# A fused cross-attention and mixture-of-experts layer: one batch's residual and moments taken apart and placed in two later steps

## The reference

```
ln      = layernorm(layernorm(x))            # x: 16 x 256 x 256, the latents
xn      = layernorm(ctx)                     # ctx: 16 x 256 x 256
q       = ln @ Wq;  k, v = split(concat(xn, ln) @ Wkv)     # 8 heads of 128, 512 keys
x       = x + tanh(g_xattn) * (softmax(q k^T / sqrt(128)) v) @ Wo + bo
h       = layernorm(x)                       # rows of the router and the experts
gates   = h @ Wg;  the two largest of 8, softmax over the two
x       = x + tanh(g_ffn) * sum over the two of w * (silu(h @ W1[e]) @ W2[e])
```

## Time and profile before

| what | value |
|---|---|
| median of 3 runs | 1544.16 us (1540.41 to 1545.47) |
| the profiled execution | 1537.72 us |
| its span, first to last instruction | 1536.0 us |
| busy share PE / PEld / DVE / ACT / POOL | 98% / 90% / 72% / 62% / 39% |
| one batch in the attention stage (8 steps) | 66.4 us, to 0.05 us the same from batch to batch |

### The profile page before, as it was taken

How to read it: one execution, slowest core, us unless ns; L and a number is a source line. 1 busy time by engine, 2 the same in 40 slices (tenths; PEclk the granted TensorE clock), 3 DMA queues, 4 the chain that set the end, 5 groups by cost and what they waited for, 6 DMA issues and landing times. The chain is left out here.

```text
span 1536.0 us, 29968 instructions
## 1 busy us (share of the span) xinstructions
PE 1499.6 (98%) x10446; PEld 1381.2 (90%) x10446; DVE 1112.4 (72%) x2689; ACT 950.0 (62%) x2057; POOL 601.7 (39%) x714
## 2 busy tenths in 40 slices
PE   8999999999999999999999999999889999999997
PEld 6889898898988888898888989888889999999996
DVE  7677777777777777777777777687796666666685
ACT  5555656556565555555565555655787777777775
POOL 5323424333342433434233342233455444444443
PEclk9999999999999999999999999999999999999999
DMA  4000100000000010000000000012855555445563
GB/s 158 10 22 8 22 8 22 28 1 29 8 22 8 22 29 8 22 8 22 8 22 28 8 22 8 8 27 85 227 126 132 129 147 141 129 126 151 136 173 83
DMA packets 57823, 91.13 MB, mean 59 GB/s; under 512 B 8617, under 2 KB 44774, under 8 KB 57550
## 3 DMA queue, kind: packets, MB, share of 16 engines
q1 hardware_dynamic: 41710, 70.19, 14.2%
q0 software_dynamic: 15824, 18.98, 7.0%
q10 hardware_dynamic: 144, 0.05, 0.0%
HBM read 70.91 MB, written 18.29 MB: 58 GB/s over the span
## 5 line engine op out<-in xcount | busy, mean ns | idle before, releaser
L885 POOL TENSOR_SCALAR probs<-probs,rsum 128x512 f32<-128x512 f32 x256 | 174.1, 692 | 532.4 <-DVE rsum L1559 532.2
L1091 ACT ACTIVATE pt_hi<-turn 128x512 fp32r<-128x512 f32 x256 | 139.1, 595 | 238.2 <-PE turn L1239 236.8
L910 POOL DMA_INDIRECT out_rows<-yo,token x71 | 121.6, 1713 | 206.7 <-DMA out_rows<-yo,token 134.5
L1676 DVE TENSOR_TENSOR ht_lo<-hs,ht_hi 128x512 fp32r<-128x512 f32 x142 | 98.2, 691 | 118.1 <-ACT ht_hi L1058 113.3
L1553 DVE TENSOR_REDUCE smax<-score 128x1 f32<-128x512 f32 x256 | 169.6, 684 | 13.1 <-PE score L189 12.7
L992 ACT ACTIVATE probs<-score,nbias 128x512 f32<-128x512 f32 x256 | 173.0, 685 | 3.9 <-DVE nbias L1555 3.8
L1049 ACT ACTIVATE hs<-ph,vecs 128x256 f32<-128x256 f32 (+1 forms) x284 | 114.1, 457 | 93.5 <-PE ph L189 82.4
L1786 DVE TENSOR_TENSOR pt_lo<-turn,pt_hi 128x512 fp32r<-128x512 f32 x256 | 164.1, 682 | 8.3 <-ACT pt_hi L1091 8.1
L187 PE MATMUL py<-w_hi,ht_lo 128*128 (+1 forms) x568 | 162.7, 286 | 3.2 <-DVE ht_lo L1676 3.2
L189 PE MATMUL py<-w_hi,ht_hi 128*128 (+1 forms) x568 | 160.6, 283 | 0.0
L188 PE MATMUL py<-w_lo,ht_hi 128*128 (+1 forms) x568 | 160.5, 283 | 0.0
(11 more groups left out here) (245 smaller groups left out, 4703.2 us busy)
## 6 DMA issues: line engine op xcount, KB each, us to landing
w_raw<-in_L_ffn_W SPq DMA_DIRECT2D x45, 1024.0 KB, 15.6
xhat_rows<-rows SPq DMA_DIRECT2D x16, 264.0 KB, 2.2
x_raw<-in_x SPq DMA_DIRECT2D x16, 256.0 KB, 3.2
c_raw<-in_ctx SPq DMA_DIRECT2D x16, 256.0 KB, 3.3
out_rows<-x SPq DMA_DIRECT2D x16, 256.0 KB, 2.5
xg<-xhat_rows,token POOLq DMA_INDIRECT x71, 4.5
out_rows<-yo,token POOLq DMA_INDIRECT x71
v_raw<-in_L_xattn_Wkv SPq DMA_DIRECT2D x2, 512.0 KB, 8.0
```

What stands on the lines that cost most here:

```text
L885: last = pool.tensor_scalar(probs[n % 2][:, t, :], probs[n % 2][:, t, :], rsum[:, n % 2, t:t + 1], 1.0, ALU.mult, ALU.mult)
L910: pool.indirect_dma_start(out=A["out"], out_offset=bass.IndirectOffsetOnAxis(ap=token[:, u:u + 1].bitcast(U32), axis=0), in_=yo_of(t)[:, s ...
L1091: act.activation(pt[0][:, 2 * t:2 * t + 2, :], turn[t][:, :].rearrange("p (j i) -> p j i", j=2), ACT.Copy).then_inc(s_pthi, 1)
```

## The change

The single function `residual` becomes three: `add_bias` (the sum into `y`), `residual` (the gate, the old `x` and `s_x2`) and `row_moments`. Only `add_bias` stays at the end of step `h == 1`. `residual` goes between `kt_lo` and `qt_lo` of step `h == 2`, `row_moments` to the same place in step `h == 3`. `norm_rows` on POOL goes from behind `normalise` of `h == 1` to behind `normalise` of `h == 3`, ahead of `prepare`. `A_STEP` becomes 4: POOL's `prepare` goes from `h == 3` to `h == 4`; DVE's moments of `x_raw` go from the end of `h == 2` to the end of `h == 3`, because they stand at `A_STEP - 1`, and the moments of `c_raw` from the end of `h == 3` to between `kt_lo` and `qt_lo` of `h == 4`. The last batch, which has no later step, runs the three functions in a row as before. PE's, ACT's and SP's loops are as they were.

```diff
-A_STEP = 3
+A_STEP = 4
 Z_STEP = 2
 R_STEP = 1
 T_STEP = 3
@@ POOL, loop over i, behind normalise(i)
+                if h == T_STEP and 1 <= b < B:
+                    norm_rows(b - 1)
                 if h == A_STEP and b + 2 < B:
                     prepare(b + 2)
                 if h == Z_STEP and b + 1 < B:
                     split_kv(b + 1)
-                if h == R_STEP and 1 <= b < B:
-                    norm_rows(b - 1)
@@ DVE
-            def residual(b):
-
+            def add_bias(b):
                 dve.wait_ge(s_proj, b + 1)
                 dve.tensor_tensor(y[:, :, :], proj[:, :].rearrange("p (t d) -> p t d", t=TT),
                                   bo[:, :].unsqueeze(1).to_broadcast([P, TT, D]), ALU.add)\
                     .then_inc(s_projr, 1)
+
+            def residual(b):
                 dve.wait_ge(s_projr, b + 1)
                 if b >= 2:
                     dve.wait_ge(s_x2st[b % 2], 16 * (b // 2))
                 dve.scalar_tensor_tensor(out=x2[b % 2][:, :, :], in0=y[:, :, :], scalar=tgate[:, 0:1],
                                          in1=x_raw[b % 3][:, :, :], op0=ALU.mult, op1=ALU.add).then_inc(s_x2, 1)
+
+            def row_moments(b):
                 dve.wait_ge(s_x2, b + 1)
                 moments("c", [x2[b % 2][:, t, :] for t in range(TT)], mv_c, s_mvc, s_xn, b)
@@ DVE, loop over i
                     if u[0] in "kq":
                         read_unit(*u)
+
+                    if u[0] == "k":
+                        if h == R_STEP + 1 and 1 <= b < B:
+                            residual(b - 1)
+                        if h == R_STEP + 2 and 1 <= b < B:
+                            row_moments(b - 1)
+                        if h == A_STEP and b + 2 < B:
+                            prepare_a(b + 2, 1)
...
-                if h in (A_STEP - 1, A_STEP) and b + 2 < B:
-                    prepare_a(b + 2, h - A_STEP + 1)
+                if h == A_STEP - 1 and b + 2 < B:
+                    prepare_a(b + 2, 0)
                 if 1 <= b < B:
-                    for at, part in ((R_STEP, residual), (G_STEP, largest), (E_STEP, choose), (W_STEP, weigh),
+                    for at, part in ((R_STEP, add_bias), (G_STEP, largest), (E_STEP, choose), (W_STEP, weigh),
                                      (L_STEP, find_places)):
...
+            add_bias(B - 1)
             residual(B - 1)
+            row_moments(B - 1)
```

## The result

| | median | runs | range |
|---|---|---|---|
| before | 1542.29 us | 4 | 1539.93 to 1545.47 |
| after | 1596.35 us | 4 | 1595.43 to 1610.06 |

The ratio is 1.037, 95% interval 1.031 to 1.043: slower by 54 us, where +53 us was forecast. The profiled execution of after took 1595.43 us, its span is 1593.7 us, 57.7 us longer than that of before. (The new functions shift lines of DVE's code behind them by one to three; POOL's and PE's lines that are shown here have kept their numbers.)

A forecast was written before the change was run, and what follows sets the result against it. PE, busy 98% of the span, was taken as the bound. -8.4 (`kt_lo` wait) + 46.5 (wait at `t`) + 14.9 (clock falls) = +53 us on the median 1544.2 gave 1597 us, range 1578 to 1610.

The forecast's parts named there:

- What the change could bring: PE's `o` in `h == 2` no longer waits for DVE's `kt_lo`: 0.56 us a batch, -8.4 us in all.
- The pieces in the gaps at no cost: Gate and moments fit DVE's 0.95 us gaps between `kt_lo` and `qt_lo` of `h == 2` to `h == 4`: cost 0.
- `norm_rows` behind `normalise` of the step of its reader: In `h == 3` PE's `t` waits for POOL's `rows`: 3.1 us in each of batches 1 to 15, +46.5 us.
- the rival of a slow one: `norm_rows` as slow as in the last batch, 1.8 us more each, 27 us on top: 1624 us; chance 0.03.
- No cost for `x_raw`: Load issued near 507 lands by 513, ahead of its reader near 518 at the end of `h == 3`: cost 0.
- The clock: PE's clock falls behind 9 of the 15 waits at `t`, about 1.65 us each: +14.9 us, an estimate.
- all fifteen would cost a fall: Rival: the clock falls behind every wait at `t`, 24.8 us in all: 1607 us; chance 0.14.

The follow-up runs named there:

- the experiment with other rows: Changed kernel, but PE's `t` of batches 1 to 14 turns the previous batch's rows, so it need not wait: 1538.9 us, 0.9962 of the kernel before.
- The kernel with `A_STEP = 3`: Changed kernel with `x2` moments at the end of `h == 2`, `norm_rows` behind `normalise` of `h == 2`, and `A_STEP` back to 3: 1542.3 us, 0.9991.
- the kernel with the filled wait: Changed kernel with 24 transposes of the unit matrix on PE ahead of its wait at `t`: 1590.08 us, 1.0291 of the kernel before.
- the fastest version: Changed kernel with `x2` moments at the end of `h == 2` and `norm_rows` behind `normalise` of `h == 2`: 1536.5 us, 0.9943 of the kernel before.

## Why the prediction was right

- **What the change could bring.** 8.4 us: `h == 2` went from 9.25 to 8.69 us, the 0.56 of the earlier trace rows, in every batch to 0.04 us; with the wait at `t` gone the whole kernel is 0.57% faster (0.35 to 0.79%). Right.
- **The pieces in the gaps at no cost.** Right: the gate left 0.29 us of the gap, the moments 0, and `h == 4` is no longer than before.
- **`norm_rows` behind `normalise` of the step of its reader.** The step that carried the forecast: 3.1 us a batch. Measured 3.08, with hand-overs of 0.08 and 0.15 us where 0.1 and 0.14 were taken. Right: `norm_rows` itself took 2.47 us (537.70 to 540.17), so the rival of a slow one is out, and the experiment with other rows shows that nothing else costs.
- **No cost for `x_raw`.** Right with `A_STEP = 4`: in after the reader, at the end of `h == 3`, never waits for the load. The kernel with `A_STEP = 3` shows what the move guards against.
- **The clock.** The least certain term, 14.9 us: measured 8 falls instead of 9, 16.3 us, five near 1.65 (69.02 to 70.65 us a batch) and three near 2.7, since the low level could last twice as long as the one stretch seen at the start. The sum was right with both parts a little off, and in the second profile of the same kernel it is seven falls. That the median came within 1 us of 1597 is partly luck: the same kernel's runs reach from 1593 to 1612. The guess at the number of falls was luck too. It was placed between two rows of one trace, the start, where the clock fell, and the wait at the end of the attention stage, where it stayed; in the trace of after both places came out the other way (last section). One trace could not tell how often such a wait lowers the clock.
- **The kernel that the Trainium skill tells of** in "TensorE: Matmul & The Clock Gate" (section "HAM oscillation — how this bites in real kernels") fell back to the half clock in every pass of its loop. Its PE waited some 3 to 5 us in each, by the same section; these waits are 2.9 us, and 8 and 7 of 15 lowered the clock. The direction agrees, but that all fifteen would cost a fall did not follow from that kernel.
- **Not in the sum:** the 2.7 us behind the attention stage. The clock fell there in after at a wait that before has too (last section), but the executions differ by more than that in this part anyway.

## What to carry to other kernels

When a piece is moved to a later place of an in-order queue, look up every reader of what it writes and compare the times, not the step numbers: here writer and reader stood in the same step of their loops, but POOL's `normalise` ends 0.36 us after PE has come to the end of its own part of the step, and the writer starts only then. A wait of 3 us in an otherwise unbroken stream of matmuls can cost more than itself, because the clock may fall behind it, and not in every run. An edit that is worth nothing alone can be what another edit needs: try them in pairs before dropping one.

## What the runs showed of the hardware beyond that

The same wait may or may not lower the clock. Where the attention stage ends PE waits 2.76 us for `xt_lo` in before as in after. Stretches right behind that wait, of before and then of after:

```profile
1082.30:1088.00 5.70, 5.70 (x48) 5.70 (x49) 4.17 (x13) 3.22 (x7) 4.48 (x5) 1.00 1.09 356
```

```profile
1137.30:1143.00 5.70, 5.70 (x27) 5.70 (x28) 3.25 (x12) 2.42 (x6) 4.48 (x5) 0.50 1.09 355
```

27 matmuls instead of 48 in the same 5.7 us. In the nine traces the clock fell there in six, that of the fastest version among them, and stayed up in three. The kernel's start is such a place as well. PE has the same two waits there, 0.94 and 0.95 us in before and 0.95 and 0.96 in after. In before the clock was 0.50 in the stretch behind them; in after it was not:

```profile
9.50:12.80 3.30, 2.59 (x23) 2.18 (x20) 2.59 (x5) 2.93 (x6) 1.33 (x1) 1.00 1.03 403
```

It fell there in four of the nine traces. What decides it is open.

DVE and ACT stood still once for a reason that the profile does not show. In the kernel with the filled wait, batch 2, DVE's timeline:

```profile
170.61 0.69 DVE L1539 TENSOR_TENSOR y<-proj,bo 128x512 f32<-128x512 f32 x1 [0.27 <-PE proj L189]
176.46 1.29 DVE L1558 TENSOR_REDUCE smax<-score 128x1 f32<-128x512 f32 x2 [5.16 <-remote]
```

ACT stood for 6.75 us beside it, PE ran out of work for 4.05 us, the clock fell there, and step `h == 2` took 15.56 instead of 8.7 us. With the same releaser, DVE stood for 0.9 to 3.3 us in `h == 2` of batch 4 in five of the other six experiments (that step is 0.6 to 2.1 us longer there), but not in the attention stage of before and after. What it is stays open; it adds some us to single executions.
